# Second cross-attention of a two-layer perceiver block: late own scores in two batches, a reordered opening, and value products ahead of scores and turning

## The chip, the cores and the metric

The kernel runs on one core of a Trainium2 chip. The metric is the device time of one execution in microseconds (us). Before the change three executions gave 468.21, 469.70 and 469.79 us, median 469.7. One more execution was taken with the profiler; it took 471.41 us, of which the profile's span covers 469.6.

## The reference

The network is six sub-layers on a residual stream `x` of 2 batches x 64 queries x 256. The change lies in the fourth, the second cross-attention. Cut to what matters:

```python
def _L1_xattn_ref(x, context, w_qkv, w_proj, b_proj):      # x (2,64,256) normed, context (2,1024,512)
    H, D = 16, 16; scale = D ** -0.5
    q, k, v = heads of x @ w_qkv.T                          # own keys and values: 64 per batch
    extra_k, extra_v = heads of context                     # 1024 per batch, used as they are
    k = concat([extra_k, k]); v = concat([extra_v, v])      # 1088 keys
    attn = softmax((q * scale) @ k.T)
    return (attn @ v) @ w_proj.T + b_proj
```

## The kernel before

The program is written by hand, one instruction stream for each engine: TensorE (PE), VectorE (DVE), ScalarE (ACT), GpSimd (POOL) and SyncE (SP) for the loads. Streams are tied by counting semaphores; each engine runs its stream strictly as written, and that order is what the change edits. No scheduler stands behind it.

**Rows.** The sixteen heads are taken as eight pairs j, with two batches b. A row r = 2j + b is one pair in one batch; the two heads of the pair with 64 queries each fill the 128 partitions. There are sixteen rows, r = 0 to 15. For each row there are these steps, and the texts below use the letters:

- S(r), `sim1` (L1962): four products of the queries with the 1024 context keys into PSUM tile `W[r % 2]`. Queries are kept as a high and a low part, so each half is multiplied twice. It waits for the exponentials of row r-2, which release that tile.
- DVE takes the row maximum of S(r) (`TENSOR_REDUCE`, L1300), joins it with the maximum of the row's own scores into the negated maximum (`TENSOR_SCALAR`, L1311).
- ACT takes the exponentials of the 1024 scores (L881) and of the 64 own scores (L883) into `probs1`.
- T(r), `turn1` (L2027): nine transposes of the probabilities, three at a time (c = 0, 1, 2) into PSUM banks 4, 5 and 7. ACT copies the thirds c = 0 and 2 to SBUF (L872), DVE the third c = 1 (L1323, called the DVE copy below). Each third waits until its bank's last contents were copied.
- A(r), `attend1` (L2045): nine value products from the copied thirds into bank 6. It waits for the two ACT copies and the DVE copy of the same row (`pt1_sbA`, `pt1_sbV`). Every fourth row a copy of bank 6 (L1286) goes to SBUF on DVE, and A(4), A(8) and A(12) wait for it.

**Order on PE.** The loop runs r from 2 to 18: S(r), then T(r-2), then A(r-3). A(q) so has T(q+1) and S(q+3) between it and T(q).

**Order on DVE.** In turn r: every fourth turn first the copy of bank 6; then the maximum and negated maximum of row r; then the DVE copy of row r-2; then, in a few turns, extra work. In order on ACT: the two copies of row r-2, then the exponentials of row r.

**Own scores.** The 64 own keys of each batch are scored apart (`own_scores`, L1980), all into bank 5. Pair 0 is done in the opening, pairs 1 to 3 before the loop, and the late pairs 4 to 7 at the end of turn r = 7: sixteen products, for which PE waits until the DVE copy of row 5 is out of bank 5 and until the low parts of the late queries are there (`q1_lo`, made on DVE at the end of turn 6, L1251). DVE then copies the scores to `work` (L1332) and takes their eight maxima (L1333), and only then may T(6) use bank 5.

**Opening.** After the turned input `xT` PE computes the queries of pair 0, the own keys, S(0) and S(1), the own values (L1997), the own scores of pair 0, the queries of pairs 1 to 7 (L1947), and the own scores of pairs 1 to 3; then the loop begins. `stay_warm(n, times)` is a run of products of a constant tile with itself into bank n whose results nobody reads.

Of the kernel before, what the change touches and what calls it, by code (L numbers as in the profile page):

```python
# [6 lines left out]
ALU = mybir.AluOpType  # L7
# [116 lines left out]


RB_BANK, O1_BANK = (0, 4), (1, 5)
RAW_BANK = (0, 1, 6, 7)
# [128 lines left out]
def perceiver_kernel(nc, x_in, ctx_in, ctxT_in, units_in, const_in, cols_in, vecs_in, rows_in, gate_in, out):  # L256
    with ExitStack() as stack:
# [231 lines left out]
        def own_scores_of(r):  # L489

            j = r // 2
            src, first = (scr[:, 5888:], 0) if j < 2 else (hn[:, :], 4) if j < 4 else (work[:, 512:], 8)
            return src[:, (r - first) * NQ:(r - first + 1) * NQ]

# [169 lines left out]
        def _(act):  # L664
# [191 lines left out]
            act.copy(KS1, bank(5).rearrange("p (m t) -> p m t", m=4)).then_inc(*tick("k1_hi"))  # L856
            act.wait_ge(*made("v1_ps"))
            act.copy(vsb[:, :], bank(4)[:, 0:DIM]).then_inc(ev("v_sb"), 1)
            act.wait_ge(ev("own_ps"), 1)
# [4 lines left out]
            for r in range(ROWT + 2):  # L864
                if r >= 2:
                    q = r - 2
                    for n, (t, bk) in enumerate(((0, 4), (6, 7))):
                        act.wait_ge(ev("pt1_ps"), 3 * q + (1, 3)[n])
                        if q >= 2:

                            act.wait_ge(ev("pv1_ps"), q - 1)
                        act.copy(PT1[q % 2][:, t:t + 3, :], bank(bk)[:, 0:3 * P].rearrange("p (t m) -> p t m", t=3))\  # L872
                            .then_inc(ev("pt1_sbA"), 1)
                if r < ROWT:
# [3 lines left out]
                    if r >= 4:  # L878
# [4 lines left out]
                    act.activation(probs1[:, r % 4, NCTX + NQ * b:NCTX + NQ * (b + 1)], own_scores_of(r), ACT.Exp,  # L883
                                   bias=negm[:, m:m + 1], accum_out=z1[:, m, 1:2]).then_inc(ev("exp1_done"), 1)
                    if r == 1:
# [106 lines left out]
        def _(dve):  # L992
# [251 lines left out]
            give(norm(x[:, :], hn[:, :], 1e-5))  # L1244

            def keep_masked_q_lo(part, js, raw):

                dve.wait_ge(*((ev("q1_hi"), 2 * part + 2) if part < 2 else (ev("q1_late_hi"), 2)))
                for h in range(2):
                    lows = QSL[0][:, js] if part < 2 else QSL[1]  # L1250
# [31 lines left out]
            for r in range(ROWT + 4):  # L1282
# [14 lines left out]
                if r < ROWT:  # L1297
# [7 lines left out]
                    if r == 2:  # L1305
# [11 lines left out]
                if 2 <= r < ROWT + 2:  # L1317
                    q = r - 2
                    dve.wait_ge(ev("pt1_ps"), 3 * q + 2)
                    if q >= 2:  # L1320
# [213 lines left out]
        def _(pe):  # L1534
# [409 lines left out]
            def query_rows(js, bk, first):  # L1944
                for j in js:
                    for k in range(KT):
                        mm = pe.matmul(bank(bk)[:, (j - first) * P:(j - first + 1) * P], WDUPQ[:, k, j, :], xT[:, k, :],  # L1947
                                       start=(k == 0), stop=(k == KT - 1))
                mm.then_inc(ev("q1_ps"), 1)

            def sim1(r):
# [4 lines left out]
                if r >= 2:  # L1956

                    pe.wait_ge(ev("exp1_done"), r - 1)
                for n, q in enumerate((QSH[:, j], QSL[j // 4][:, j % 4])):
                    for kh in range(2):  # L1960
# [7 lines left out]
            def own_scores(js):  # L1968

                for jp in range(2):  # L1970
                    rows = slice(64 * jp, 64 * jp + 64)
                    of_rows = [j for j in js if j % 2 == jp]
                    if jp == 1 and of_rows:
                        even_done[0] += 1
                        mm.then_inc(ev("own_even"), 1)
                        pe.wait_ge(ev("own_even"), even_done[0])
                    for r in [2 * j + b for j in of_rows for b in range(B)]:
                        b, j = r % 2, r // 2
                        for n, q in enumerate((QSH[:, j], QSL[j // 4][:, j % 4])):
                            mm = pe.matmul(bank(5)[:, (r % 8) * NQ:(r % 8 + 1) * NQ], q[rows, b].rearrange("p h q -> p (h q)"),  # L1980
                                           KS1[rows, j // 2, b * NQ:(b + 1) * NQ], start=(n == 0), stop=(n == 1))
# [24 lines left out]

            def turn1(r):

                pe.wait_ge(ev("exp1_done"), r + 1)
                for c in range(3):  # L2010
                    if r >= 1:
# [8 lines left out]
                    elif c == 2:  # L2020

                        pe.wait_ge(ev("q1_raw"), 1)
                    if r == 6 and c == 1:

                        pe.wait_ge(ev("own_late"), 1)
                    for t in range(3):
# [54 lines left out]
            for i in range(KT):  # L2081
# [279 lines left out]
```

## Time and profile before

| what | us |
|---|---|
| median of three executions (468.21 to 469.79) | 469.7 |
| profiled execution, its own time | 471.41 |
| its span | 469.6 |
| PE busy | 449.0 (96%) |
| DVE busy | 259.3 (55%) |
| ACT busy | 242.4 (52%) |
| second cross-attention, from the turned input at 317.7 to the output products at 378.4 | 60.7 |

PE times are modelled ends of pipelined products, so the starts are the firmer numbers: the distance from one S to the next is the length of a row. "[0.17 <-ACT scr L872]" behind a row is the idle time of the engine ahead of it, and what ended it; "issue" means nothing that the profile shows.

### The profile page before, as it was taken

The page shows a single profiled execution, that of the slowest core. Times are in us where ns is not written, and L with a number is a line of the kernel's source. Part 1 is how long each engine was busy: PE and PEld are TensorE (multiplying, and loading weights), DVE is VectorE, ACT ScalarE, POOL GpSimd, SP SyncE. Part 2 cuts the span into 40 slices and gives each one's busy share as a digit, 9 for nine tenths or more (in the row PEclk, how much of TensorE's full clock was granted, in tenths as well). Part 3 has the DMA queues.
Part 4 walks back from the last instruction along what each step waited for, and adds up shares of the span by engine and source line. Part 5 has one row for each costly group of instructions (what it writes and reads, how often), then busy time and mean ns, then how long its engine had stood idle before and what let it go on. Part 6 is the DMA issues. An engine that isn't in the chain of part 4 may idle for free.

```text
span 469.6 us, 8537 instructions
## 1 busy us (share of the span) xinstructions
PE 449.0 (96%) x3506; PEld 389.6 (83%) x3506; DVE 259.3 (55%) x465; ACT 242.4 (52%) x444; POOL 127.4 (27%) x115
## 2 busy tenths in 40 slices
PE   8999999999999999999988999999989999999997
PEld 7887989899997989899966678997666779778797
DVE  2657223244526142222046788975776866469996
ACT  2577333264545343242124768765857865347872
POOL 1110000002000500000020477979900000019795
PEclk9999999999999999999999999999888999999999
DMA  8924810005200060059990688990000394260220
GB/s 284 411 94 187 289 71 1 1 0 191 80 0 1 13 231 39 1 222 282 215 351 7 242 340 325 355 359 2 2 1 1 130 426 165 90 268 1 86 95 13
DMA packets 15303, 68.95 MB, mean 147 GB/s; under 512 B 1429, under 2 KB 3877, under 8 KB 9504
## 3 DMA queue, kind: packets, MB, share of 16 engines
q1 hardware_dynamic: 13184, 60.60, 36.2%
q0 software_dynamic: 2080, 7.80, 4.7%
q8 instruction: 28, 0.46, 0.4%
q14 instruction: 11, 0.09, 0.1%
HBM read 64.07 MB, written 4.33 MB: 146 GB/s over the span
## 4 chain that ended last, share of the span: by engine, by line
PE 75%; DVE 8%; ACT 6%; POOL 5%; issue 3%; DMA 1%; SPq 0%; DVEq 0%; ACTq 0%; POOLq 0%
PE W L1665 20%; PE W L1621 15%; PE W L1824 8%; POOL w_lo L589 5%; PE W L1905 4%; PE W L2027 3%; PE W L1638 3%; PE W L1962 2%; PE W L2045 2%; PE W L1687 2%; DMA fixed<-units_dram 1%; PE W L1544 1%; DVE small L1300 1%; PE W L1925 1%; PE W L1980 1%
## 5 line engine op out<-in xcount | busy, mean ns | idle before, releaser
L1665 PE MATMUL W<-probs_turned_hi,ctx_split_hi 128*128 128x256 f32 x256 | 72.9, 285 | 2.5 <-issue 2.5
L1665 PE MATMUL W<-probs_turned_hi,ctx_split_lo 128*128 128x256 f32 x256 | 72.5, 283 | 0.0
L1665 PE MATMUL W<-probs_turned_lo,ctx_split_hi 128*128 128x256 f32 x256 | 72.5, 283 | 0.0
L589 POOL TENSOR_TENSOR w_lo<-arena,w_hi 128x320 fp32r<-128x320 f32 (+1 forms) x38 | 56.5, 1511 | 19.2 <-ACT w_hi L677 18.9
L1072 DVE TENSOR_TENSOR probs_turned_lo<-W,probs_turned_hi 128x512 fp32r<-128x512 f32 x32 | 20.6, 686 | 64.2 <-ACT probs_turned_hi L737 64.2
L1035 DVE TENSOR_TENSOR w_lo<-arena,w_hi 128x704 fp32r<-128x704 f32 (+1 forms) x40 | 49.1, 1256 | 6.3 <-ACT w_hi L677 5.8
L1665 PEld LDWEIGHTS W<-probs_turned_hi,ctx_split_hi 128*128 128x128 f32 x256 | 49.1, 192 | 3.7 <-issue 3.3
L598 POOL TENSOR_TENSOR small<-small,const 128x1 f32<-128x1 f32 (+2 forms) x10 | 7.0, 697 | 166.0 <-DVE small L1153 75.3
L1665 PEld LDWEIGHTS W<-probs_turned_lo,ctx_split_hi 128*128 128x128 f32 x256 | 49.1, 192 | 0.2
L1665 PEld LDWEIGHTS W<-probs_turned_hi,ctx_split_lo 128*128 128x128 f32 x256 | 49.1, 192 | 0.0
L677 ACT CAST w_hi<-arena 128x1024 fp32r<-128x1024 f32 x40 | 41.7, 1049 | 13.3 <-PE W L1905 6.9
L756 ACT ACTIVATE pbuf<-W,small 128x1024 f32<-128x1024 f32 x16 | 17.9, 1116 | 59.5 <-DVE small L1092 59.5
L1905 PE MATMUL W<-w_hi,acts 128*128 128x256 f32 x240 | 44.3, 286 | 0.0
L1621 PE MATMUL W<-ctx_turned_hi,q_keys_hi 128*128 128x512 f32 x128 | 41.1, 402 | 0.5 <-DVE q_keys_lo L1065 0.5
L1621 PE MATMUL W<-ctx_turned_lo,q_keys_hi 128*128 128x512 f32 x128 | 39.7, 391 | 0.0
L1621 PE MATMUL W<-ctx_turned_hi,q_keys_lo 128*128 128x512 f32 x128 | 39.6, 390 | 0.0
L1905 PEld LDWEIGHTS W<-w_hi,acts 128*128 128x128 f32 x240 | 38.4, 191 | 0.1
L748 ACT COPY scr<-W 128x256 f32<-128x256 f32 x32 | 11.8, 367 | 48.9 <-PE W L1665 48.9
L589 POOL TENSOR_TENSOR w_lo<-ctxmem,w_hi 128x320 fp32r<-128x320 f32 (+1 forms) x22 | 32.8, 1510 | 10.9 <-ACT w_hi L677 10.6
L1905 PE MATMUL W<-w_lo,acts 128*128 128x256 f32 x120 | 33.9, 283 | 0.0
L1084 DVE TENSOR_REDUCE small<-W 128x1 f32<-128x1024 f32 x16 | 19.6, 1223 | 25.5 <-PE W L1621 25.5
L1824 PE MATMUL W<-w_hi,acts 128*128 128x512 f32 x104 | 33.5, 398 | 0.1
(428 smaller groups left out, 928.3 us busy)
## 6 DMA issues: line engine op xcount, KB each, us to landing
arena<-units_dram SPq DMA_DIRECT2D x27, 1024.0 KB, 6.2
ctxmem<-units_dram SPq DMA_DIRECT2D x11, 1024.0 KB, 8.8
fixed<-units_dram SPq DMA_DIRECT2D x6, 1024.0 KB, 6.8
ctxsplit<-kept_keys SPq DMA_DIRECT2D x8, 512.0 KB, 19.5
pbuf<-ctx_dram POOLq DMA_DIRECT2D x4, 512.0 KB, 6.2
kept_keys<-ctx_turned_hi SPq DMA_DIRECT2D x2, 1024.0 KB, 9.5
kept_keys<-ctx_turned_lo SPq DMA_DIRECT2D x2, 1024.0 KB, 11.5
ctxmem<-ctx_dram SPq DMA_DIRECT2D x2, 1024.0 KB, 13.3
```

The lines of the kernel that those rows point to most:

```text
L589: pool.tensor_tensor(w_slot(1, p)[:, lo:hi], half_in(p)[:, lo:hi], f32(w_slot(0, p)[:, lo:hi]), ALU.subtract).then_inc(ev("lo_by_gpsimd"), 1)
L677: act.copy(w_slot(0, p), half_in(p)).then_inc(ev(hi_done(p)[0]), 1)
L756: act.activation(probs0[:, r % 2, :], W[r % 2][:, :], ACT.Exp, bias=negm[:, r:r + 1], accum_out=stat[:, r, 1:2]).then_inc(ev("exp_done"), 1)
L1035: dve.tensor_tensor(w_slot(1, p)[:, lo:hi], half_in(p)[:, lo:hi], f32(w_slot(0, p)[:, lo:hi]), ALU.subtract).then_inc(ev("lo_by_vector"), 1)
L1072: dve.tensor_tensor(PT[1][at], bank(4 + c).rearrange("p (t m) -> p t m", t=4), f32(PT[0][at]), ALU.subtract).then_inc(ev("pl_sb"), 1)
L1084: step(dve.tensor_reduce(mx[:, r % 2:r % 2 + 1], W[r % 2][:, :], AX_X, ALU.max))
L1621: mm = pe.matmul(W[r % 2][:, kh * 512:(kh + 1) * 512], QP[a][:, c, j, :], CXT[z][:, c, kh * 512:(kh + 1) * 512], start=(c == 0 and n == 0) ...
L1638: mm = pe.transpose(bank(4 + c)[:, t * P:(t + 1) * P], probs0[:, r % 2, (4 * c + t) * P:(4 * c + t + 1) * P], ident)
L1665: mm = pe.matmul(ps, CXN[a][:, t, c * P:(c + 1) * P], PT[z][:, t, :], start=(t == 0 and n == 0), stop=(t == KEYT - 1 and n == 2))
L1824: mm = pe.matmul(bank(4 + hf), XS[a][:, e, k, :], w_slot(z, p)[:, hf * 512:(hf + 1) * 512], start=u == "m1e0" and k == 0 and n == 0, stop= ...
L1905: mm = pe.matmul(bank(n % (E + 1) % 4)[:, 0:DIM], UTS[a][:, t, :], w_slot(z, p)[:, (t % 4) * DIM:(t % 4 + 1) * DIM], start=(t == 0 and i = ...
L2027: mm = pe.transpose(bank((4, 5, 7)[c])[:, t * P:(t + 1) * P], probs1[:, r % 4, (3 * c + t) * P:(3 * c + t + 1) * P], ident)
```

## The change

It has four parts, all inside the second cross-attention.

1. The late own scores are made in two batches of eight products: pairs 4 and 6 in the turn of row 4 (r = 6), pairs 5 and 7 in the turn of row 6 (r = 8), between S(r) and T(r-2). In these two turns the transposes go in the order c = 0, 2, 1. ACT copies each batch to `work`, and DVE takes its four maxima. The low parts of the late queries are made in two halves, in the turns r = 4 and 5.
2. The opening: the queries of pairs 1 to 3 come directly behind S(1), then the own scores of pair 0, the late queries, the own values, four constant products, S(2), and only then the own scores of pairs 1 to 3. ACT copies the own values between the exponentials of rows 0 and 1.
3. In each turn PE runs A(r-3), then S(r), then T(r-2).
4. The places of the late queries in their tiles follow the new batches (`QUERIES`).

```diff
+OWN_LATE = (4, 6)
+QUERIES = (0, 1, 2, 3, 4, 6, 5, 7)
...
# ACT
+                    if q in OWN_LATE:
+                        odd = OWN_LATE.index(q)
+                        act.wait_ge(ev("own_ps"), 3 + odd)
+                        act.wait_ge(ev("rows2_split"), 2)
+                        act.copy(work[:, 512 + 256 * odd:768 + 256 * odd], bank(5)[:, 0:4 * NQ]).then_inc(ev("own_late"), 1)
                     for n, (t, bk) in enumerate(((0, 4), (6, 7))):
-                        act.wait_ge(ev("pt1_ps"), 3 * q + (1, 3)[n])
+                        act.wait_ge(ev("pt1_ps"), 3 * q + (1, 3 if q not in OWN_LATE else 2)[n])
...
# DVE
+                    if r in (8, 10):
+                        dve.wait_ge(ev("ownmax_late"), r // 2 - 3)
...
-                if r == 6:
-                    keep_masked_q_lo(2, slice(4, 8), QRAW)
-                if r == 7:
-                    dve.wait_ge(ev("rows2_split"), 2)
-                    dve.wait_ge(ev("own_ps"), 3)
-                    step(dve.tensor_copy(work[:, 512:], bank(5)))
-                    dve.tensor_reduce(ownmax[:, 8:], work[:, 512:].rearrange("p (r q) -> p r q", q=NQ), AX_X, ALU.max)\
-                        .then_inc(ev("own_late"), 1)
+                if r in (4, 5):
+                    keep_late_q_lo(r - 4)
+                if r - 2 in OWN_LATE:
+                    odd = OWN_LATE.index(r - 2)
+                    dve.wait_ge(ev("own_late"), odd + 1)
+                    late = work[:, 512 + 256 * odd:768 + 256 * odd]
+                    dve.tensor_reduce(ownmax[:, 8:].rearrange("p (i n b) -> p n i b", n=2, b=B)[:, odd],
+                                      late.rearrange("p (i b q) -> p i b q", i=2, b=B), AX_X, ALU.max)\
+                        .then_inc(ev("ownmax_late"), 1)
...
# PE, opening
             sim1(0)
             sim1(1)
+            query_rows(range(1, 4), 6, 1)
+            pe.wait_ge(*made("k1_lo"))
+            own_scores((0,))
+            query_rows(QUERIES[4:], 7, 0)
             for k in range(KT):
                 mm = pe.matmul(bank(4)[:, 0:DIM], xT[:, k, :], wx[:, k, 512:768], start=(k == 0), stop=(k == KT - 1))
             mm.then_inc(*tick("v1_ps"))
-            pe.wait_ge(*made("k1_lo"))
-            own_scores((0,))
-            query_rows(range(1, 4), 6, 0)
-            query_rows(range(4, 8), 7, 4)
             pe.wait_ge(ev("self_sb"), 1)
+            stay_warm(5, 4)
             pe.wait_ge(ev("q1_lo"), 4)
+            sim1(2)
             own_scores((1, 2, 3))
...
# PE, loop
             for r in range(2, ROWT + 3):
-                if r < ROWT:
+                if r >= 3:
+                    attend1(r - 3)
+                if 3 <= r < ROWT:
                     sim1(r)
+                if r - 2 in OWN_LATE:
+
+                    odd = OWN_LATE.index(r - 2)
+                    pe.wait_ge(ev("pt1_sbV"), r - 2)
+                    if odd == 0:
+                        pe.wait_ge(ev("q1_lo"), 8)
+                    own_scores((4 + odd, 6 + odd))
                 if 2 <= r < ROWT + 2:
                     turn1(r - 2)
-                if r >= 3:
-                    attend1(r - 3)
-                if r == 7:
-
-                    pe.wait_ge(ev("pt1_sbV"), 6)
-                    pe.wait_ge(ev("q1_lo"), 6)
-                    own_scores((4, 5, 6, 7))
```

How the streams stand, first PE where the loop begins. Before, L1962 is S, L2027 is T and L2045 is A (eight products with context values, one with own values); the piece holds S(3), T(1), A(0), S(4), T(2), A(1).

```order
L1962 MATMUL W<-ctxsplit,acts 128x512 x4
L2027 MATMUL W<-const,pbuf 128x128 x9
L2045 MATMUL W<-scr,ctxmem 32x128 x8
L2045 MATMUL W<-scr,vsb 32x128
L1962 MATMUL W<-ctxsplit,acts 128x512 x4
L2027 MATMUL W<-const,pbuf 128x128 x9
L2045 MATMUL W<-scr,ctxmem 32x128 x8
L2045 MATMUL W<-scr,vsb 32x128
```

Now L1985 is S, L2053 is T and L2071 is A; the piece holds T(0), A(0), S(3), T(1), A(1).

```order
L2053 MATMUL W<-const,pbuf 128x128 x9
L2071 MATMUL W<-scr,ctxmem 32x128 x8
L2071 MATMUL W<-scr,vsb 32x128
L1985 MATMUL W<-ctxsplit,acts 128x512 x4
L2053 MATMUL W<-const,pbuf 128x128 x9
L2071 MATMUL W<-scr,ctxmem 32x128 x8
L2071 MATMUL W<-scr,vsb 32x128
```

The rows look alike, but a T is now followed by the A of the same row; before, it was followed by the A of the row ahead.

Next PE's opening, between the own keys and T(0). Before: L1962 is S(0) and S(1), L1997 the own values, L1980 own scores, L1947 queries.

```order
L1962 MATMUL W<-ctxsplit,acts 128x512 x8
L1997 MATMUL W<-arena,xT 128x256 x2
L1980 MATMUL W<-acts 128x64 x4
L1947 MATMUL W<-xT,ctxmem 128x128 x14
L1980 MATMUL W<-acts 128x64 x12
L1962 MATMUL W<-ctxsplit,acts 128x512 x4
```

Now, with L1969 the queries, L2004 own scores, L2025 own values and L1566 the constant products:

```order
L1985 MATMUL W<-ctxsplit,acts 128x512 x8
L1969 MATMUL W<-xT,ctxmem 128x128 x6
L2004 MATMUL W<-acts 128x64 x4
L1969 MATMUL W<-xT,ctxmem 128x128 x8
L2025 MATMUL W<-arena,xT 128x256 x2
L1566 MATMUL W<-const 128x128 x4
L1985 MATMUL W<-ctxsplit,acts 128x512 x4
L2004 MATMUL W<-acts 128x64 x12
```

S(2) moved ahead of the own scores of pairs 1 to 3, and four constant products stand ahead of it.

Last DVE in the turns r = 6 and 7. Before: maximum, negated maximum and DVE copy of turn 6, the low queries (L1251), the copy of bank 6 (L1286), the same three of turn 7, and copy and maxima of the late own scores.

```order
L1300 TENSOR_REDUCE small<-W 128x1
L1311 TENSOR_SCALAR small<-small 128x1
L1323 COPY scr<-W 128x384
L1251 SCALAR_TENSOR_TENSOR ctxsplit<-ctxmem,small,acts 128x8x64 x2
L1286 COPY ctxmem<-W 128x512
L1300 TENSOR_REDUCE small<-W 128x1
L1311 TENSOR_SCALAR small<-small 128x1
L1323 COPY scr<-W 128x384
L1332 COPY work<-W 128x512
L1333 TENSOR_REDUCE small<-work 128x8
```

Now (L1319, L1332 and L1344 are maximum, negated maximum and DVE copy, L1354 the four maxima of a batch, L1305 the copy of bank 6):

```order
L1319 TENSOR_REDUCE small<-W 128x1
L1332 TENSOR_SCALAR small<-small 128x1
L1344 COPY scr<-W 128x384
L1354 TENSOR_REDUCE small<-work 128x2x2
L1305 COPY ctxmem<-W 128x512
L1319 TENSOR_REDUCE small<-W 128x1
L1332 TENSOR_SCALAR small<-small 128x1
L1344 COPY scr<-W 128x384
```

The low queries and the 128x512 copy of own scores are gone from here; the DVE copy of a row still stands behind the maximum of the row two ahead.

## Rows read from the trace of the kernel before

**Rows 1.** The page: busy PE; the chain that ended last, by engine.
```profile
PE 449.0 (96%) x3506; PEld 389.6 (83%) x3506; DVE 259.3 (55%) x465; ACT 242.4 (52%) x444; POOL 127.4 (27%) x115
...
PE 75%; DVE 8%; ACT 6%; POOL 5%; issue 3%; DMA 1%; SPq 0%; DVEq 0%; ACTq 0%; POOLq 0%
```

**Rows 2.** Timeline, turn r = 6: start, us, engine, line, what, count, idle before.
```profile
339.45 0.73 PE L1962 MATMUL W<-ctxsplit,acts 64*128 64x512 f32 x4
340.12 1.20 PE L2027 MATMUL W<-const,pbuf 128*128 128x128 f32 x9
340.23 1.23 DVE L1300 TENSOR_REDUCE small<-W 128x1 f32<-128x1024 f32 x1 [0.63 <-PE W L1962]
...
341.25 0.64 PE L2045 MATMUL W<-scr,ctxmem 128*32 128x128 f32 x16
341.36 0.48 ACT L872 COPY scr<-W 128x384 f32<-128x384 f32 x1 [0.18 <-PE W L2027]
341.49 0.21 DVE L1311 TENSOR_SCALAR small<-small 128x1 f32<-128x1 f32 x1
...
341.62 0.55 DVE L1323 COPY scr<-W 128x384 f32<-128x384 f32 x1
...
342.02 0.73 PE L1962 MATMUL W<-ctxsplit,acts 64*128 64x512 f32 x4
```

**Rows 3.** Timeline, the late own scores and the rows behind them.
```profile
342.08 1.41 DVE L1251 SCALAR_TENSOR_TENSOR ctxsplit<-ctxmem,small,acts 128x512 fp32r<-128x512 f32 x2
...
343.41 0.68 DVE L1286 COPY ctxmem<-W 128x512 f32<-128x512 f32 x1
...
344.24 0.65 PE L2045 MATMUL W<-scr,ctxmem 128*32 128x128 f32 x16 [0.35 <-DVE ctxmem L1286]
...
345.39 0.55 DVE L1323 COPY scr<-W 128x384 f32<-128x384 f32 x1
...
345.99 0.29 PE L1980 MATMUL W<-acts 64*128 64x64 f32 x1 [0.94 <-DVE scr L1323]
...
347.60 0.49 PE L1962 MATMUL W<-ctxsplit,acts 64*128 64x512 f32 x1
...
351.31 1.08 PE L2045 MATMUL W<-scr,ctxmem 128*32 128x128 f32 x16
...
352.73 0.80 PE L1962 MATMUL W<-ctxsplit,acts 64*128 64x512 f32 x2
...
353.88 2.18 PE L2027 MATMUL W<-const,pbuf 128*128 128x128 f32 x9
...
356.76 0.51 PE L1962 MATMUL W<-ctxsplit,acts 64*128 64x512 f32 x2
```

**Rows 4.** Windows: us, busy time by engine, granted clock, DMA share, GB/s.
```profile
336.90:339.45 2.55, 2.55 (x32) 1.82 (x31) 1.96 (x4) 2.37 (x7) 2.26 (x5) 1.00 0.01 3
...
350.00:352.70 2.70, 2.70 (x24) 1.93 (x24) 1.52 (x3) 1.29 (x2) 0.00 (x0) 0.50 0.03 6
```

**Rows 5.** Timeline, the opening and S(3).
```profile
321.24 1.13 PE L1997 MATMUL W<-arena,xT 128*128 128x256 f32 x4
...
322.86 3.39 PE L1947 MATMUL W<-xT,ctxmem 128*128 128x128 f32 x28
...
324.50 1.05 ACT L849 ACTIVATE acts<-W,small 128x384 fp32r<-128x384 f32 x2 [1.27 <-PE W L1947]
...
326.88 1.40 PE L1980 MATMUL W<-acts 64*128 64x64 f32 x9 [0.63 <-DVE acts L1251]
...
330.83 0.41 DVE L1309 TENSOR_REDUCE small<-hn 128x4 f32<-128x256 f32 x1
...
331.50 0.98 PE L1962 MATMUL W<-ctxsplit,acts 64*128 64x512 f32 x4
```

**Rows 6.** Timeline, S(15), and A(14) with A(15) behind it.
```profile
369.61 0.50 PE L1962 MATMUL W<-ctxsplit,acts 64*128 64x512 f32 x2
...
375.42 0.64 PE L2045 MATMUL W<-scr,ctxmem 128*32 128x128 f32 x16
...
376.06 0.64 PE L2045 MATMUL W<-scr,ctxmem 128*32 128x128 f32 x16
```

More of the change, by code:

```diff
@@ L489, in own_scores_of @@
         def own_scores_of(r):
-            j = r // 2
-            src, first = (scr[:, 5888:], 0) if j < 2 else (hn[:, :], 4) if j < 4 else (work[:, 512:], 8)
-            return src[:, (r - first) * NQ:(r - first + 1) * NQ]
+            j, b = r // 2, r % 2
+            src, at = (scr[:, 5888:], r) if j < 2 else (hn[:, :], r - 4) if j < 4 else \
+                (work[:, 512:], 4 * (j % 2) + 2 * (j // 2 - 2) + b)
+            return src[:, at * NQ:(at + 1) * NQ]
         block = stack.enter_context(nc.Block())
@@ L856, in _ @@
             act.copy(KS1, bank(5).rearrange("p (m t) -> p m t", m=4)).then_inc(*tick("k1_hi"))
-            act.wait_ge(*made("v1_ps"))
-            act.copy(vsb[:, :], bank(4)[:, 0:DIM]).then_inc(ev("v_sb"), 1)
             act.wait_ge(ev("own_ps"), 1)
@@ L884, in _ @@
                                    bias=negm[:, m:m + 1], accum_out=z1[:, m, 1:2]).then_inc(ev("exp1_done"), 1)
+                    if r == 0:
+                        act.wait_ge(*made("v1_ps"))
+                        act.copy(vsb[:, :], bank(4)[:, 0:DIM]).then_inc(ev("v_sb"), 1)
                     if r == 1:
@@ L1244, in _, with keep_late_q_lo @@
             give(norm(x[:, :], hn[:, :], 1e-5))
+            def keep_late_q_lo(jp):
+                dve.wait_ge(ev("q1_late_hi"), 2)
+                at = slice(2 * jp, 2 * jp + 2)
+                for h in range(2):
+                    dve.scalar_tensor_tensor(out=QSL[1][:, at, :, h, :],
+                                             in0=QRAW[:, at].rearrange("p j (b q) -> p j b q", b=B),
+                                             scalar=hmask[:, h:h + 1], in1=f32(QSH[:, 4:8][:, at, :, h, :]),
+                                             op0=ALU.mult, op1=ALU.subtract).then_inc(ev("q1_lo"), 1)
             def keep_masked_q_lo(part, js, raw):
-                dve.wait_ge(*((ev("q1_hi"), 2 * part + 2) if part < 2 else (ev("q1_late_hi"), 2)))
+                dve.wait_ge(ev("q1_hi"), 2 * part + 2)
                 for h in range(2):
-                    lows = QSL[0][:, js] if part < 2 else QSL[1]
+                    lows = QSL[0][:, js]
                     dve.scalar_tensor_tensor(out=lows[:, :, :, h, :], in0=raw.rearrange("p j (b q) -> p j b q", b=B),
@@ L1318, in _ @@
                     q = r - 2
-                    dve.wait_ge(ev("pt1_ps"), 3 * q + 2)
+                    dve.wait_ge(ev("pt1_ps"), 3 * q + (2 if q not in OWN_LATE else 3))
                     if q >= 2:
@@ L1944, in query_rows @@
             def query_rows(js, bk, first):
-                for j in js:
+                for i, j in enumerate(js):
                     for k in range(KT):
-                        mm = pe.matmul(bank(bk)[:, (j - first) * P:(j - first + 1) * P], WDUPQ[:, k, j, :], xT[:, k, :],
+                        mm = pe.matmul(bank(bk)[:, (first + i) * P:(first + i + 1) * P], WDUPQ[:, k, j, :], xT[:, k, :],
                                        start=(k == 0), stop=(k == KT - 1))
@@ L1958, in sim1 @@
                     pe.wait_ge(ev("exp1_done"), r - 1)
-                for n, q in enumerate((QSH[:, j], QSL[j // 4][:, j % 4])):
+                at = QUERIES.index(j)
+                for n, q in enumerate((QSH[:, at], QSL[at // 4][:, at % 4])):
                     for kh in range(2):
@@ L1972, in own_scores @@
                     of_rows = [j for j in js if j % 2 == jp]
-                    if jp == 1 and of_rows:
+                    if jp == 1 and of_rows and len(js) == 3:
                         even_done[0] += 1
@@ L1978, in own_scores @@
                         b, j = r % 2, r // 2
-                        for n, q in enumerate((QSH[:, j], QSL[j // 4][:, j % 4])):
-                            mm = pe.matmul(bank(5)[:, (r % 8) * NQ:(r % 8 + 1) * NQ], q[rows, b].rearrange("p h q -> p (h q)"),
+                        at, i = (r if j < 4 else 2 * (j // 2 - 2) + b) * NQ, QUERIES.index(j)
+                        for n, q in enumerate((QSH[:, i], QSL[i // 4][:, i % 4])):
+                            mm = pe.matmul(bank(5)[:, at:at + NQ], q[rows, b].rearrange("p h q -> p (h q)"),
                                            KS1[rows, j // 2, b * NQ:(b + 1) * NQ], start=(n == 0), stop=(n == 1))
@@ L2009, in turn1 @@
                 pe.wait_ge(ev("exp1_done"), r + 1)
-                for c in range(3):
+                for c in (0, 1, 2) if r not in OWN_LATE else (0, 2, 1):
                     if r >= 1:
@@ L2022, in turn1 @@
                         pe.wait_ge(ev("q1_raw"), 1)
-                    if r == 6 and c == 1:
-                        pe.wait_ge(ev("own_late"), 1)
+                    if r in OWN_LATE and c == 1:
+                        pe.wait_ge(ev("own_late"), OWN_LATE.index(r) + 1)
                     for t in range(3):
```

## The prediction

> **What bounds the kernel now.** I read the page first: PE is busy for 449.0 of 469.6 us and makes up 75% of the chain that ended last [rows 1]. So a change pays where it shortens PE's stream or its waits, and costs where it makes PE wait. Then the timeline of one quiet row of the second cross-attention [rows 2]. S(6) starts at 339.45, T(4) at 340.12, A(3) at 341.25, S(7) at 342.02: a row takes 2.57 us, in three stretches of 0.67 (S to T), 1.13 (T to A) and 0.77 us (A to the next S). PE pauses for no other engine there. DVE runs behind S in the same row: its maximum starts 0.78 us after S and takes 1.23 (339.45 to 340.23 to 341.46), the negated maximum starts at 341.49, the DVE copy of T(4) runs from 341.62 to 342.17. ACT's second copy runs from 341.36 to 341.84. A(3), at 341.25, uses copies of T(3) made a row earlier. That distance is why the copies cost nothing today: A(4) comes only after S(7) and T(5).
>
> Third, the timeline behind this row [rows 3]. S(7) to S(8) takes 5.58 us, S(8) to S(9) 5.13, S(9) to S(10) 4.03 (from 342.02, 347.60, 352.73, 356.76), together 7.0 us over three quiet rows. This is the stall around the late own scores. Fourth, the windows: PE's clock is at 1.00, its upper level of 2.4 GHz, in the quiet row, and at 0.50, 1.2 GHz, at 350.0 to 352.7 [rows 4].
>
> **Loop order, the large term.** Now A(q) stands directly behind T(q) on PE, and so waits for three copies which A once found ready. DVE's order is the same: maximum of S(r), negated maximum, DVE copy of T(r-2). I take S(r)'s start as zero and use rows 2. The maximum starts at 0.78; the negated maximum follows at 2.04 and the DVE copy at 2.17, ending at 2.72. The third of T that it copies is long there (T starts at 0.67 and ends at 1.87). ACT's second copy ends at 2.39, before it. The step from the end of a DVE copy to PE's start is 0.05 us in one row (345.94 to 345.99) and 0.15 us in another (344.09 to 344.24) [rows 3]; I take 0.10. A starts at 2.82, and S(r+1) 0.77 later, at 3.59. A row takes 3.59 instead of 2.57 us: PE stands for 1.0 us between T and A. Nothing else on PE fills this time, since the next S is queued behind the waiting A; and ACT and DVE get their next row later by as much. What this order gives back is nothing I can find: S(r) waits for the exponentials of row r-2, and in rows 2 it starts 0.77 us behind A with no wait.
>
> **The rows S(3) to S(15)**, twelve steps of 3.59 us, are 43.1. Four of them are longer:
> - S(6) to S(7): eight own products stand between S(6) and T(4). The rows show sixteen from 345.99 to the next S at 347.60, and nine in 1.40 us in the opening [rows 3, 5]; I take 0.95 for eight. T(4) ends at about 2.82 instead of 1.87, the DVE copy at 3.45. Then on DVE come the four maxima (0.41, as over the same 256 columns in rows 5) and the copy of bank 6 (0.68), for which A(4) waits. A(4) starts at 4.6, S(7) at 5.4: +1.8.
> - S(8) to S(9): own products and the DVE copy behind them, no copy of bank 6: +0.7. ACT's copy of a batch (128x256) lies beside T's first two thirds.
> - S(10) to S(11): A(8) waits for two small DVE sums (0.38 together) and the copy of bank 6 (0.68): +1.1. S(14) to S(15): A(12) waits for that copy: +0.7.
>
> The sum is 43.1 + 1.8 + 0.7 + 1.1 + 0.7 = 47.4 us. Before, S(3) at 331.50 to S(15) at 369.61 was 38.1 [rows 5, 6]. So +9.3: the late own scores give back 5.4 us or so, and the waits eat it and much more. The low late queries cost nothing: before 1.41 us in one piece [rows 3], now two halves, each in the 1.65 us that DVE stands between its copy's end at 2.72 and the next maximum at 4.37. Without that cover they would cost at most 1.41.
>
> **The opening.** After S(1), at 321.24, PE has the same 28 query steps (3.39 us) and the own values (1.13) [rows 5], pair 0's own scores (0.6), and eight more steps of constant products at the queries' pace of 0.12 (1.0). With 0.2 of gaps S(2) starts at 327.5. The low queries of pairs 1 to 3 don't hold it: ACT makes the high ones in 1.05 us after pair 0's own copy, about 323.9 to 324.9, and DVE is done by 327. S(2) takes 0.7, the twelve own products 1.5, ACT's two copies of them end at 330.45. Then two maxima, the negated maximum and the DVE copy of T(0) (0.3, 0.41, 0.2, 0.55) bring A(0) to 332.05 and S(3) to 332.8. Before, S(3) was at 331.50: +1.3, though A(0) now is behind it.
>
> **The tail.** After S(15): A(13) at 2.82, T(14) at 3.59, 1.2 us of T, an ACT copy (0.48) and 0.1 us on either side of it, A(14) at 5.45, T(15) at 6.3, again T and copy, A(15) at 8.2. Before it was 376.06 - 369.61 = 6.45 [rows 6]. So +1.75. What follows is unchanged and hangs on A(15); the weight loads that wait for S(15) move with it.
>
> **Sum:** 1.3 + 9.3 + 1.75 = 12.4 us, with 11.6 for the step of 0.05 and 13.2 for that of 0.15. The profiled execution took 471.4 us, 1.7 over the median, so it becomes 483.8 and the median 482.1. I forecast 482.
>
> **The clock.** In rows 4 the clock fell to 1.2 GHz behind the stretch of own scores, where PE did short products and stood for DVE (0.94 us ahead of the first). In my sum PE is at 2.4 GHz throughout, though the loop now makes it stand for 1.0 us in each 3.59. At 1.2 GHz T takes 2.18 us, S to T 1.15 and A to S 1.42 [rows 3]. One slow stretch as in the trace costs 1 to 2 us; I add none to the forecast and keep some four for the range. The Trainium skill, TensorE: Matmul & The Clock Gate, A second HAM failure mode: psum-queue depth-cycling, says that small idle spells of PE between groups of products, once per iteration, can make the clock swing between its levels. The same page, Loop structure matters more than you think, says that a DVE copy out of PSUM between the groups doesn't cool PE. By the second the sum stays 12.4; by the first it would be up to 36 at the worst; no run here yet shows this loop, and quiet rows with PE fully busy can't decide it.
>
> **Rivals.**
> - *The clock halves in the loop.* A row would then be S to T 1.15, T 2.18, an ACT copy with its steps 0.68, A to S 1.42: 5.43 us, 1.84 more than 3.59. All thirteen rows slow add 24 us, 506; half of them 494. For it: the clock fell twice in this stage. Against: at the lower level PE would be busy for 4.75 of 5.43 us, and in the trace such busy stretches bring the clock back (it is at 1.00 again by 356.76, where S and T follow one another without a pause). Chance 0.14, for anything over 488.
> - *The wait is short, and the late own scores decide.* If the copies were ready for A(q), the rows S(3) to S(15) would be 12 x 2.57 + 1.9 (sixteen own products) = 32.7, 5.4 less than now, the opening +0.5, the tail 0: 4.9 less, 465 for the median. The place is the start of A; it decides from a wait under 0.38 us in each of thirteen rows. For it: the 7.0 us of stall are real [rows 3]. Against: the DVE copy alone takes 0.55 us and begins after the maximum of the next S, in the order that DVE still has. Chance 0.05.
> - *A shorter wait.* If DVE's copy came before ACT's, A would start at 2.49 and a row be 3.26: thirteen rows give 4 us back, 478 or less, down to the no-change case. It needs DVE to be faster than any row shows. Chance 0.08, with 0.02 of it within half a per cent.
>
> **How the numbers follow.** The forecast, 478 to 488, has 0.73; 0.14 is above, 0.13 below. The range of 477 to 490 takes in some of either side and holds a little over 0.8. Half a per cent is 2.3 us, about what a measurement of this kernel can tell from no change. Faster 0.05, within it 0.02, slower 0.93.
>
> **What would show it.** In the new trace, quiet rows of about 3.6 us from S to S; A ahead of which PE stands about 0.9 us with the DVE copy as what ended it; DVE's maximum no longer waiting behind its own work but for S; the turn r = 6 at about 5.4 us; S(2) at 327.5 and S(3) at 332.8; A(15) at about 388; the clock at 1.00 in most of the loop. I am wrong if A is released by ACT or not at all, if rows stay under 3 us, or if the clock is at 0.50 in more than two spells.

## The result and the profile after

The changed kernel takes 485.27 us, median of four executions (484.65 to 486.58); the kernel before, on the same chip, 469.75 (468.21 to 471.92). The ratio is 1.032, with an interval of 1.028 to 1.035: slower, by 15.5 us. The execution that was profiled took 484.65 us, 13.2 more than the one of before. Medians and ratios in this document leave out three executions that ran slow at a much lower mean granted clock, one of experiment 7 (509.79 us at 0.947) and two of the kernel before (495.84 at 0.85, 724.69 at 0.559).

On the page, PE is still busy for about the same time [rows 1], in a longer span:

```profile
PE 447.7 (93%) x3514; PEld 389.7 (81%) x3514; DVE 262.2 (54%) x467; ACT 243.5 (50%) x446; POOL 127.3 (26%) x115
...
PE 73%; DVE 12%; ACT 6%; POOL 5%; issue 3%; DMA 0%; DVEq 0%; POOLq 0%; ACTq 0%
```

DVE's share of the chain went from 8 to 12%. A quiet row in the timeline, the answer to [rows 2], from S(7) to S(8) (L1985 is S, L2053 T, L2071 A, L1344 the DVE copy):

```profile
350.37 0.74 PE L1985 MATMUL W<-ctxsplit,acts 64*128 64x512 f32 x4
...
351.04 1.20 PE L2053 MATMUL W<-const,pbuf 128*128 128x128 f32 x9
351.15 1.23 DVE L1319 TENSOR_REDUCE small<-W 128x1 f32<-128x1024 f32 x1 [1.67 <-PE W L1985]
...
352.27 0.48 ACT L878 COPY scr<-W 128x384 f32<-128x384 f32 x1 [0.18 <-PE W L2053]
352.41 0.21 DVE L1332 TENSOR_SCALAR small<-small 128x1 f32<-128x1 f32 x1
352.54 0.55 DVE L1344 COPY scr<-W 128x384 f32<-128x384 f32 x1
...
353.23 0.65 PE L2071 MATMUL W<-scr,ctxmem 128*32 128x128 f32 x16 [0.99 <-DVE scr L1344]
...
353.98 0.50 PE L1985 MATMUL W<-ctxsplit,acts 64*128 64x512 f32 x2
```

The row takes 3.61 us. T ends, ACT's second copy ends at 352.75, the DVE copy at 353.09, and A starts 0.14 later; PE stood for 0.99 us, and the row names the DVE copy. The maximum, which in before stood 0.63 us for S [rows 2], now stands 1.67: DVE has time to spare and is still what PE waits for, because the copy is queued behind the maximum. The chain that ended last runs through the same loop (start, us, what):

```profile
358.92 1.24 DVE small L1319
360.21 0.10 issue
360.31 0.56 DVE scr L1344
360.87 0.14 issue
361.00 0.81 PE W L2071 x18
361.82 0.68 PE W L1985 x4
```

Maximum, copy, A, S, maximum: T is not in it. Summed over the stage (window 318 to 400 of the groups by line; after the bar busy us and mean ns, then idle us ahead and what ended it):

```profile
L2071 PE MATMUL W<-scr,ctxmem 128*32 128x128 f32 x256 | 10.3, 277 | 17.7 <-DVE scr L1344 10.7 <-DVE ctxmem L1305 5.3 <-ACT scr L878 1.7
```

and the same group before:

```profile
L2045 PE MATMUL W<-scr,ctxmem 128*32 128x128 f32 x256 | 10.7, 287 | 0.4 <-DVE ctxmem L1286 0.4
```

The wait of PE ahead of A grew from 0.4 to 17.7 us. The clock did not fall in it: the granted clock is 1.00 (columns as in [rows 4]: length, busy time of PE, PEld, DVE, ACT and POOL with counts, granted clock, DMA share, GB/s), and T takes 1.20 us, as in the quiet row of before, and not the 2.18 of its slow stretch [rows 3].

```profile
330.00:384.00 54.00, 37.54 (x434) 27.41 (x433) 34.98 (x57) 33.48 (x85) 11.44 (x10) 1.00 0.02 5
```

**Where the 13.2 us between the two profiled executions lie.** From the first query product to the output products the stage took 60.74 us before (317.69 to 378.43) and 72.69 after (318.99 to 391.68): +11.95. What follows the output products takes 91.1 to 91.2 us in every trace. The stage began 1.3 us later, and that is no part of the change: the whole offset is there by 9.6 us, in the identical start of the program. The same six constant products took 0.94 us in before and 1.65 after (one line of each timeline), and products behind them went on at the slower pace until 9.5 us:

```profile
5.84 0.94 PE L1544 MATMUL W<-const 128*128 128x128 f32 x6 [0.46 <-ACT xT L670]
```

```profile
6.16 1.65 PE L1566 MATMUL W<-const 128*128 128x128 f32 x6 [0.46 <-ACT xT L673]
```

Over all traces of this study the stage began between 317.5 and 319.9 us. So I compare stages as well as times below. The medians differ by 2.3 us more than the profiled executions: before's profiled one lay 1.7 above its median and after's 0.6 below.

The granted clocks on record account for part of this. The trace of before ran at half rate for 10.2 us of the stage (328.7 to 332.1 and 349.2 to 356.0), and its mean granted clock is 0.989. Of 42 later executions of the same kernel, on the chips of the experiments, 33 had 0.993, with a median of 470.4 us, which is a third less time at half rate, and six had 0.989, with a median of 472.2. So the stage of 60.74 us is probably 1 to 2 us longer than in most executions (an estimate from these medians). The loss is then larger by as much than the traces show, and the gains against before that are read from stages below are smaller. Of the changed kernel's four executions two had a mean clock of 1.00 (484.65, the profiled one, and 484.79), one 0.996 (485.75) and one 0.993 (486.58).

### The profile page after: what moved, and what is told of

Read it like the earlier page. It is cut to its first block, busy times and chain, and to the rows that moved or that the text cites. A ratio compares the mean times of both kernels' runs of the same rounds, so it can differ in the third digit from the quotient of the medians.

```text
span 482.8 us, 8561 instructions
## 1 busy us (share of the span) xinstructions
PE 447.7 (93%) x3514; PEld 389.7 (81%) x3514; DVE 262.2 (54%) x467; ACT 243.5 (50%) x446; POOL 127.3 (26%) x115
## 4 chain that ended last, share of the span: by engine, by line
PE 73%; DVE 12%; ACT 6%; POOL 5%; issue 3%; DMA 0%; DVEq 0%; POOLq 0%; ACTq 0%
PE W L1687 19%; PE W L1643 15%; PE W L1846 7%; POOL w_lo L592 5%; PE W L1927 4%; DVE small L1319 3%; PE W L1660 3%; PE W L2071 2%; PE W L1985 2%; PE W L1709 2%; PE W L1566 2%; DVE scr L1344 1%; PE W L2053 1%; PE W L1595 1%; PE W L1947 1%
```

## The experiments

The first line says what was changed, against which kernel. "Stage" is the distance from the first query product to the output products in the profiled execution: 60.74 before, 72.69 after. Ratios are to executions of the kernel before on the same chip as the run: median 471.73 us for experiments 1 to 4, 470.24 for 5 to 7, 471.09 for 8 and 9. Experiment 2 has the line numbers of before; in 4, 5 and 9 the line numbers are one higher than in the changed kernel.

**1. The old loop order in the changed kernel.** Everything else of the change stays.

```diff
             for r in range(2, ROWT + 3):
-                if r >= 3:
-                    attend1(r - 3)
...
                     turn1(r - 2)
+                if r >= 3:
+                    attend1(r - 3)
```

> The changed kernel with one edit: the loop runs S(r), late own scores, T(r-2), A(r-3) as before the change; opening and two batches stay. Theory (the loss is PE's wait between T(q) and the A(q) directly behind it): quiet rows fall from 3.60 to 2.57 us, A is released without a wait, S(3) to S(15) is 12 x 2.57 + 2 x 0.95 = 33 us (48.0 in the changed kernel, 38.1 before), the last stretch S(15) to A(15) is 6.45 again. Total about 464 us, 463 to 467, faster than before by 1%. Rival (the loss comes from the new opening or from the late batches' longer path over ACT and DVE): rows stay above 3.2 us and the total stays at 480 or more.

Measured: 470.70 us (469.07 to 471.12), ratio to before 0.998 (0.9966 to 0.9996), stage 58.73. The order accounts for 14.0 us of stage, more than the whole loss; A's wait is gone:

```profile
L2071 PE MATMUL W<-scr,ctxmem 128*32 128x128 f32 x256 | 10.7, 288 | 0.0
```

But I had expected the late batches to bring 4 to 8 us, and the stage shows 2.0. S(6) to S(7) takes 7.45 us there. Its timeline:

```profile
340.72 1.90 POOL L658 TENSOR_TENSOR arena<-arena,cols 128x1024 f32<-128x1024 f32 x1
...
341.35 1.95 DVE L1260 SCALAR_TENSOR_TENSOR ctxsplit<-ctxmem,small,acts 128x256 fp32r<-128x256 f32 x2
...
343.44 0.27 PE L2004 MATMUL W<-acts 64*128 64x64 f32 x1 [2.59 <-DVE ctxsplit L1260]
```

PE stands 2.59 us for the low queries, which take 1.95 us for a half beside a GpSimd instruction, where before both halves in one piece took 1.41 alone [rows 3]. Behind it the clock is at the lower level. Two windows, the stretch of the stand and the one behind it:

```profile
341.00:344.40 3.40, 0.96 (x8) 0.96 (x8) 3.40 (x4) 1.53 (x4) 1.62 (x1) 1.00 0.00 0
344.90:348.30 3.40, 3.40 (x29) 2.37 (x27) 1.51 (x3) 2.39 (x6) 0.00 (x0) 0.50 0.00 0
```

**2. The new loop order alone, in the kernel before.** Late own scores in one piece, old opening.

```diff
+                if r >= 3:
+                    attend1(r - 3)
                 if r < ROWT:
                     sim1(r)
                 if 2 <= r < ROWT + 2:
                     turn1(r - 2)
-                if r >= 3:
-                    attend1(r - 3)
```

> The kernel before with one edit: in the loop A(r-3) stands ahead of S(r) and T(r-2); late own scores in one piece in turn 7 and the old opening stay. Theory: quiet rows of 3.6 us with A released by the DVE copy, the stall of the late own scores stays and overlaps the waits of two or three rows; total 479 to 485 us, about 12 over before. Rival (the order alone costs little, and only together with the new batches does the DVE chain get long): total under 474 us and quiet rows under 3.0 us.

Measured: 490.48 us (490.19 to 490.70), ratio 1.040 (1.038 to 1.041), stage 77.40, so +16.7 and above the expected range. The rows are 3.6 us, and A's wait is there with the same releasers:

```profile
L2045 PE MATMUL W<-scr,ctxmem 128*32 128x128 f32 x256 | 11.2, 295 | 17.1 <-DVE scr L1323 7.7 <-DVE ctxmem L1286 6.5 <-ACT scr L872 2.9
```

The part I missed: in the profiled execution the clock fell here in three spells of the stage (from 356.2, 369.8 and 386.9), the second in the middle of the loop, far behind the own scores:

```profile
369.80:373.20 3.40, 3.40 (x18) 2.29 (x13) 1.91 (x3) 0.48 (x1) 0.00 (x0) 0.50 0.00 0
```

**3. S(r), A(r-3), T(r-2): one S between T and A of the same row.**

```diff
+                if r >= 3:
+                    attend1(r - 3)
                 if 2 <= r < ROWT + 2:
                     turn1(r - 2)
-                if r >= 3:
-                    attend1(r - 3)
```

(against experiment 1)

> The changed kernel with the loop order S(r), late own scores, A(r-3), T(r-2): A still stands ahead of its turn's T, but S(r) now lies between T(r-3) and A(r-3). Theory: the copies of T(r-3) are done by the time S(r) ends (ACT's about 0.58 us after S starts, DVE's 0.33, S takes 0.67), so A waits at most 0.1 us and quiet rows are 2.57 to 2.7 us; total 463 to 468 us, within 0.5% of the run with the order put back. Rival (A needs a whole row of distance, T(q+1) too, or A ahead of T delays the exponentials): quiet rows over 3.1 us, total over 474 us.

Measured: 473.64 us (473.07 to 474.56), ratio 1.004 (1.003 to 1.006), stage 62.64. The quiet rows are 2.57 to 2.78 us, so 0.67 us of S is nearly all the cover that A needs for its copies; the wait on the DVE copy is gone:

```profile
L2071 PE MATMUL W<-scr,ctxmem 128*32 128x128 f32 x256 | 10.6, 285 | 4.0 <-DVE ctxmem L1305 2.1 <-ACT scr L878 1.7 <-DVE scr L1344 0.2
```

It missed both the total of 463 to 468 and "within 0.5%" of experiment 1 (it is 0.6% above): A still stands 2.1 us for copies of bank 6, PE 2.2 for the low queries, and the tail, where no S follows, is 8.7 us from S(15) to A(15) as against 6.45 before [rows 6].

**4. The changed kernel, with GpSimd and VectorE kept apart.** DVE adds `b_proj` in turn 9 instead of 3, and GpSimd starts its weight scaling only when the low queries are done.

```diff
+                    pool.wait_ge(ev("q1_lo"), 8)
                     wo = unit("mb2")[:, KT * DIN:].rearrange("p (k n) -> p k n", k=XST)
...
-                if r == 3:
+                if r == 9:
                     step(dve.tensor_tensor(x[:, :], x[:, :], v_("b_proj"), ALU.add))
```

> The changed kernel with two DVE/GpSimd neighbours taken apart: x + b_proj moves from turn 3 to turn 9, and GpSimd's scaling of the weights (1.90 us) waits until the low parts of the late queries are done. Theory (in the changed kernel these DVE instructions took 2.32 us and 2.26 us, against 0.41 and some 0.85, because they ran beside a two-input GpSimd instruction): they return to about 0.4 and 0.9 us, S(4) to S(5) falls from 4.20 to 3.6 and S(5) to S(6) from 4.02 to 3.6, total about 1.0 us less than the changed kernel. Rival (they are slow for what they read or write): they stay over 2 us and nothing moves.

One execution: 483.52 us, stage 72.85. Where it acts, it does what was said: both halves of the low queries take 0.87 us (the first is shown), `x + b_proj` in its new place 0.41, and S(3) to S(6) start at 332.14, 335.75, 339.35, 342.96, rows of 3.60.

```profile
338.38 0.87 DVE L1261 SCALAR_TENSOR_TENSOR ctxsplit<-ctxmem,small,acts 128x256 fp32r<-128x256 f32 x2
```

The 1.0 us that this gains was given back by a spell at the lower clock that the changed kernel's trace does not have, behind the 2.11 us that PE stands ahead of A(8), where the changed kernel stands 2.04:

```profile
363.30:366.70 3.40, 3.32 (x26) 2.28 (x27) 0.67 (x1) 0.00 (x0) 0.00 (x0) 0.50 0.00 0
```

**5. Experiments 1 and 4 together** (both edits as shown).

> The changed kernel with the loop order S, T, A put back and, besides, x + b_proj moved from turn 3 to turn 9 and GpSimd's scaling of the weights held until the low parts of the late queries are done. With the order alone put back, PE stood 2.6 us ahead of the first late own scores (S(6) to S(7) took 7.45 us and the clock fell there), released by DVE's low queries of 1.91 and 1.95 us beside GpSimd. Theory (this stand, not the batches themselves, ate the gain that was expected of that run): S(6) to S(7) falls to about 3.6 us, no half-rate spell in the loop, total 4 us less than with the order alone put back: 466 us, 464.5 to 467.5, about 1.1% under the kernel before. Rival (the stand comes from late queries that are late anyway, by the multiplications on GpSimd and by the DVE's place in the turn): S(6) to S(7) stays over 5 us, total 469 or more.

Measured: 468.22 us (466.39 to 469.96), ratio 0.994 (0.992 to 0.997), stage 57.29. That is 1.4 us of stage under experiment 1, where I had expected 4, and the time lies above the expected range. S(6) to S(7) takes 5.63 us, over the 5 that the rival named. PE still stands 1.21 us ahead of the first batch. The first half of the low queries still met a GpSimd instruction and took 1.66 us, which is 0.79 of the 1.21 (an estimate: 1.66 less the 0.87 of the second half); the other 0.4 is left to the rival, the place of the low queries in DVE's turn. The clock still fell behind the stand in this trace (342.8 to 346.2), but not in every execution: seven of the twelve had a mean granted clock of 1.00, the profiled one 0.996.

```profile
334.88 2.37 POOL L652 TENSOR_TENSOR bias_rows<-work,bias_rows 8x1024 fp32r<-8x1024 f32 x1
...
336.40 1.66 DVE L1261 SCALAR_TENSOR_TENSOR ctxsplit<-ctxmem,small,acts 128x256 fp32r<-128x256 f32 x2
...
340.85 0.26 PE L2005 MATMUL W<-acts 64*128 64x64 f32 x1 [1.21 <-DVE ctxsplit L1261]
```

**6. Experiment 5 with the old opening.**

```diff
-            query_rows(range(1, 4), 6, 1)
-            pe.wait_ge(*made("k1_lo"))
-            own_scores((0,))
-            query_rows(QUERIES[4:], 7, 0)
...
             mm.then_inc(*tick("v1_ps"))
+            pe.wait_ge(*made("k1_lo"))
+            own_scores((0,))
+            query_rows(range(1, 4), 6, 1)
+            query_rows(QUERIES[4:], 7, 0)
             pe.wait_ge(ev("self_sb"), 1)
-            stay_warm(5, 4)
             pe.wait_ge(ev("q1_lo"), 4)
-            sim1(2)
```

> The same as the run with order put back and GpSimd held apart, but with the opening of the kernel before (own values, own scores of pair 0, queries, own scores of pairs 1 to 3, S(2) in the loop). It isolates the opening. Theory: the half-rate spell at S(2) and T(0) comes back, S(3) is 0.8 to 1.5 us later after the turned input (13.8 against about 13.0 us), total about 467, 1 us more than with the new opening. Rival (the new opening gains nothing, its constant products cost what the clock saves): no difference in total, or less.

Measured: 467.27 us (466.33 to 468.65), ratio 0.993 (0.990 to 0.995), stage 57.29, the same as experiment 5. (ACT's copy of the own values, which is not shown, moves back too, and S(2) goes back into the loop.) The rival came true: the new opening brings nothing and costs nothing once the loop order is back. S(3) comes 12.53 us after the first query product against 13.05 in experiment 5, but S(4) 15.60 against 15.65. The spell at S(2) and T(0) that I expected did not come back: the granted clock is 1.00 from 326 to 332 us, and T(0) takes 1.20 us, against 2.18 in the trace of before with the same opening.

**7. The changed kernel with the DVE copy ahead of the maximum.** The copy of bank 6 moves a turn ahead as well.

```diff
             for r in range(ROWT + 4):
-                if r >= 7 and r % 4 == 3 and r < ROWT:
+                if 2 <= r < ROWT + 2:
+                    q = r - 2
...
+                    dve.tensor_copy(PT1[q % 2][:, 3:6, :], bank(5)[:, 0:3 * P].rearrange("p (t m) -> p t m", t=3))\
+                        .then_inc(ev("pt1_sbV"), 1)
+                if r >= 6 and r % 4 == 2 and r < ROWT:
...
-                if 2 <= r < ROWT + 2:
-                    q = r - 2
...
```

> The changed kernel with its loop order, but on DVE the copy of T(r-2) (and every fourth turn the copy of bank 6) stands ahead of the maximum of S(r). Theory (in the changed kernel A is released by the DVE copy, which waits behind the maximum): A is now released by ACT's copy or, where the later maximum makes the exponentials late, by ACT still busy with them; quiet rows 3.3 to 3.5 us instead of 3.6, the waits of A(4), A(8), A(12) for bank 6 stay; total 1 to 4 us less than the changed kernel. Rival (the DVE copy isn't what A waits for): rows of 3.6 us and the same total.

Measured: 482.37 us (481.30 to 486.91, three executions), ratio 1.029 (1.023 to 1.035): by time it can't be told from the change. The stage is 2.4 us shorter (70.32), but 1.6 of that lie in S(10) to S(11) and S(14) to S(15), where the copy of bank 6 moved ahead. The releaser has changed as the theory wants:

```profile
L2071 PE MATMUL W<-scr,ctxmem 128*32 128x128 f32 x256 | 10.3, 278 | 14.4 <-ACT scr L878 10.3 <-DVE ctxmem L1313 3.4 <-DVE scr L1308 0.7
```

ACT's second copy is now the last of the three. Of the rows without own scores five are still 3.62 or 3.63 us, four 3.20 to 3.50 and one 3.97, where I had expected 3.3 to 3.5: the later maximum delays ACT's exponentials, and its copies stand behind them (one A is released at 359.23 by copies that ACT began at 358.33, right behind exponentials for which it had waited 1.77 us on DVE). This order on DVE did not remove PE's wait; what removed it here was work between T and A on PE (experiments 1 and 3).

**8. Experiment 1 with the batches a turn later.**

```diff
-OWN_LATE = (4, 6)
+OWN_LATE = (5, 7)
```

> The run with the loop order S, T, A put back, and each batch of late own scores one turn later (turns r = 7 and 9 instead of 6 and 8); GpSimd is left as it is. Theory (what was left of the loss with the order put back is PE's stand ahead of the first batch for the low late queries, made on DVE one turn ahead): by turn 7 they have been done for a row even at 1.9 us apiece, the stand of 2.6 us goes, each batch costs its 0.95 us, S(7) to S(8) is about 3.5 us, and no half-rate spell follows; total 465 to 467, about 1% under the kernel before. Rival (the half-rate spell comes from the short own products whatever stands ahead of them): the spell stays, S(7) to S(8) over 4.5 us, total 468 or more.

Measured: 467.11 us (466.38 to 469.14), ratio 0.993 (0.991 to 0.996), stage 56.14. PE no longer waits for the low queries, and the clock stays up in this trace, so the rival's spell is absent; but S(7) to S(8) is 5.04 us, not the 3.5 expected, since the low queries beside GpSimd (1.94 us) hold up DVE's maximum and copy instead (PE stands 1.39 us):

```profile
344.69 0.29 PE L2004 MATMUL W<-acts 64*128 64x64 f32 x1 [1.39 <-DVE scr L1344]
```

**9. Experiments 5 and 8 together.**

> The same with GpSimd held apart and x + b_proj in turn 9 as in the earlier run. Theory: DVE's low queries take 0.87 to 1.7 us, S(4) to S(7) are quiet rows of 2.57, S(7) to S(8) 3.5; total within 0.7 us of the run without it, 464 to 466.5. Rival: DVE beside GpSimd still sets rows 4 to 7 in the run without it, and this one is 1 us or more faster.

Measured: 467.21 us (465.28 to 467.60), ratio 0.991 (0.989 to 0.994), stage 55.03: 5.7 us under before, the shortest of all. S(7) to S(8) is 3.97 us, quiet rows are 2.57, and the clock is up throughout the stage:

```profile
344.07 0.29 PE L2005 MATMUL W<-acts 64*128 64x64 f32 x1 [0.33 <-DVE scr L1345]
```

```profile
329.00:372.00 43.00, 42.30 (x497) 31.53 (x497) 35.61 (x63) 36.60 (x96) 13.05 (x11) 1.00 0.11 39
```

By time it can't be told from experiment 8 (its stage began at 319.6, that of experiment 8 at 319.1); by the stage it is 1.1 us shorter, which is what the rival said of it. Its time lies above the expected 464 to 466.5. Both beat the kernel before by 0.7 to 0.9%.

## Why the prediction was right, and where its terms were off

**The large term held, in mechanism and size.** Forecast: rows of 3.59 us with PE standing 1.0 us between T and A, ended by the DVE copy. Measured: 3.60, 0.99, the DVE copy. That the order of the three steps does it, and not the batches or the opening, is shown from three sides: order back, no wait (experiment 1); order alone, the whole wait (2); one S between T and A, no wait on that copy (3). That this copy is late because of its place behind the maximum is shown by 7: moved ahead, it accounts for 0.7 us of A's wait instead of 10.7. The wait itself passes to ACT there, so the place of the DVE copy is not all of it.

**The sum.** 12.4 us were forecast for the stage and 11.95 measured, from terms that were off both ways, so that the closeness of the two sums is partly luck:

| step | forecast, us | measured, us |
|---|---|---|
| opening, to S(3) | +1.3 | +0.65 (13.81 to 14.46) |
| S(3) to S(15) | +9.3 | +9.85 (38.11 to 47.96) |
| of it S(6) to S(7), over a quiet row | 1.8 | 1.49 |
| S(8) to S(9) | 0.7 | 0.56 |
| S(10) to S(11) | 1.1 | 1.05 |
| S(14) to S(15) | 0.7 | 0.60 |
| S(4) to S(6), not in the sum | 0 | 1.02 |
| tail, S(15) to A(15) | +1.75 | +1.46 (6.45 to 7.91) |

The opening holds some luck of its own. Its +0.65 is against a trace of before with a half-rate stretch at S(2) and T(0); against experiment 6, the same old opening without that stretch (12.53 us to S(3)), it would be +1.93.

**The step that failed** is "the low late queries cost nothing", each half lying in the 1.65 us that DVE stands. They took 2.26 us for the first half and made S(5) to S(6) 0.42 us longer than a quiet row. `x + b_proj` a row earlier, which the sum leaves out, took 2.32 and made S(4) to S(5) 0.60 longer. Both ran beside a GpSimd instruction:

```profile
335.75 2.37 POOL L652 TENSOR_TENSOR bias_rows<-work,bias_rows 8x1024 fp32r<-8x1024 f32 x1
336.08 2.32 DVE L1347 TENSOR_TENSOR x<-x,vecs 128x256 f32<-128x256 f32 x1
...
339.97 1.90 POOL L658 TENSOR_TENSOR arena<-arena,cols 128x1024 f32<-128x1024 f32 x1
340.29 2.26 DVE L1260 SCALAR_TENSOR_TENSOR ctxsplit<-ctxmem,small,acts 128x256 fp32r<-128x256 f32 x2
...
344.31 0.87 DVE L1260 SCALAR_TENSOR_TENSOR ctxsplit<-ctxmem,small,acts 128x256 fp32r<-128x256 f32 x2
```

The second half, with GpSimd idle, took 0.87. In before, the same addition of `b_proj` was issued 0.07 us ahead of its GpSimd neighbour and took 0.41:

```profile
334.38 0.41 DVE L1326 TENSOR_TENSOR x<-x,vecs 128x256 f32<-128x256 f32 x1
334.45 2.57 POOL L649 TENSOR_TENSOR bias_rows<-work,bias_rows 8x1024 fp32r<-8x1024 f32 x1
```

Experiment 4 took the neighbour away and got 0.87 for both halves, 0.41 for the addition, and rows of 3.60. The Trainium skill, SBUF — State Buffer, Who interferes with whom, says that a VectorE instruction with two SBUF inputs contends with a GpSimd instruction that reads SBUF, and that the order of issue decides who blocks. These rows agree: 2.32 and 2.26 us when GpSimd came first, 0.41 when it came second.

**Where the gain of the late batches went.** The rival "the wait is short" put it at 4.9 us of stage. With the old order back only 2.0 came (experiment 1); 5.7 came with the batch a turn later and the two engines apart (9). The difference was PE's stand for the low queries and the half-rate stretch behind it. The stand came from the slowed DVE instructions and, by some 0.4 us in experiment 5, from their place in the turn. That the half-rate stretch follows from the stand is not shown: PE stood 1.21 us ahead of the batch in experiment 5 and the clock fell, and 1.39 us in experiment 8 and it stayed up. By time the gain over before is smaller than by the stage, 0.9% or some 4 us for experiment 9, as the stage of before is a long one.

**The clock.** The rival that it halves in the loop did not come true in the changed kernel: 54 us with 1.0 us of stand in each 3.60 stayed at 1.00. Two of its executions had a mean clock of 0.996 and 0.993, and where it fell in them no trace shows; but the slowest took only 1.9 us more than the profiled one, far from the 24 of a loop at half rate. The sentence of the Trainium skill that the prediction weighed for this rival (TensorE: Matmul & The Clock Gate, A second HAM failure mode: psum-queue depth-cycling) does not describe this loop's rows. It is not safe from it either: experiment 2 had three spells in the stage, 1, 3, 5 and 6 had one behind the first own scores of the loop, 4 had one behind a stand of 2.11 us, while the changed kernel's S(10) to S(11), 4.65 us with a stand of 2.04, had none. Even one kernel does both from execution to execution (experiment 5). What tells those apart stays open.

**The time** came out at 485.3, not 482, with the stage 0.45 us shorter than forecast. What is missing lies outside it, in the start of the program (1.3 us in the profiled pair), and in the step from the profiled execution to the median: the forecast took off 1.7 us, by which before's profiled execution lay over its median, but the changed kernel's lay 0.6 under its own.

## What to carry to other kernels

When engines run strictly in order, look for what stands between a producer's product and its consumer on the waiting engine: one S of 0.67 us there hid nearly all of a wait that cost 1.0 us in every row without it. Look also at the queue of the engine that makes the copy, since an idle engine can still be late when the copy stands behind something that comes later. A cover counted in idle time holds only if the covered instruction keeps its duration: before moving a two-input DVE instruction, see what GpSimd runs at the place where it will land.

## What had not been expected

The same DVE instruction took 0.41 or 2.32 us by an order of issue that differed by 0.4 us. And the beginning of the stage varied by 2.3 us between traces (317.52 to 319.86), in work that no kernel here changes, as much as several of the effects measured; comparing stages within a trace separated them where times could not.

The variation is that of TensorE's pace in the first 13 us. Behind them all eleven traces need 306.7 to 306.8 us to the stage. In six traces the products run at full pace from about 5 us or earlier, 0.11 us from start to start, and the stage begins at 317.5 to 318.1; in three (after, experiments 1 and 8) they run at 0.21 until 9.3 to 10.0, in two (2 and 9) they fall back to 0.21 from 7.5 or 8.0 on, and the stage begins at 319.0 to 319.9. The granted clock shows only the second kind. The same stretch in before, after and experiment 9 (columns as in [rows 4]):

```profile
7.50:10.00 2.50, 2.50 (x25) 2.50 (x24) 0.49 (x1) 1.54 (x2) 0.00 (x0) 1.00 1.00 315
```

```profile
7.50:10.00 2.50, 2.50 (x15) 2.43 (x15) 0.11 (x1) 1.04 (x1) 0.00 (x0) 1.00 0.94 294
```

```profile
7.50:10.00 2.50, 2.45 (x11) 2.46 (x12) 0.13 (x1) 1.04 (x1) 0.00 (x0) 0.50 1.02 330
```

After has 15 products there where before has 25, at half the pace for most of it, and its column says 1.00. In the first 10 us of these traces the column can't be relied on, and the spacing of the products tells the pace.
